# Softmax kept in PSUM, rotation finished in SBUF, and the work of five engines dealt out anew

## The reference

```python
xn = layernorm(x)
q, k, v = xn @ wq, xn @ wk, xn @ wv                 # 8 heads of 128
q, k = rope(q), rope(k)                             # halves: [e*cos - o*sin, e*sin + o*cos]
s = q @ k.T / 128 - 1e30 * (i < j)                  # causal
attn = softmax(s) @ v @ wo                          # summed over the heads
h = relu(s0 * [xn, -xn] @ sign(k0)) * 2             # 512 -> 1024
h = relu(s1 * h @ sign(k1)) * 2                     # 1024 -> 1024
out = x + attn + s2 * h @ sign(k2)                  # 1024 -> 256
```

## Time and profile before

| | us |
|---|---|
| median of three runs | 1775.95 (1774.67 to 1776.29) |
| the profiled execution | 1776.42 |
| its span, first to last instruction | 1774.5 |
| PE busy | 1721.9 (97%), 12720 matmuls |
| DVE busy | 1532.1 (86%) |
| ACT busy | 1267.3 (71%) |
| POOL busy | 927.4 (52%) |
| granted TensorE clock, mean | 0.996 of full speed |

### The profile page before, as it was taken

The page is one execution under the profiler, slowest core; times in us unless marked ns, Lnnn a source line. Parts: engine busy times, 40 slices in busy tenths (PEclk is TensorE's granted clock), DMA queues, the critical chain, the costliest instruction groups (busy, mean ns, idle before and its releaser), DMA issues.

```text
span 1774.5 us, 34051 instructions
## 1 busy us (share of the span) xinstructions
PE 1721.9 (97%) x12720; PEld 1195.5 (67%) x12720; DVE 1532.1 (86%) x3630; ACT 1267.3 (71%) x2717; POOL 927.4 (52%) x952
## 2 busy tenths in 40 slices
PE   6899989999999999999999999999999999999999
PEld 2456757767676676767767677676766767677667
DVE  7899888897988979888897988989889798888975
ACT  6677676776867777677776767768677776777763
POOL 6555545555545645464564555555456454655632
PEclk9999999999999999999999999999999999999999
DMA  4234543344343443344344343433434344343433
GB/s 172 48 48 79 93 68 79 66 78 76 63 92 58 87 70 64 86 67 85 59 79 89 63 81 66 78 72 66 87 65 88 67 65 85 67 87 58 80 70 73
DMA packets 454839, 134.09 MB, mean 76 GB/s; under 512 B 434704, under 2 KB 453648, under 8 KB 454672
## 3 DMA queue, kind: packets, MB, share of 16 engines
q1 hardware_dynamic: 454672, 131.90, 39.4%
HBM read 14.94 MB, written 8.39 MB: 13 GB/s over the span
## 4 chain that ended last, share of the span: by engine, by line
PE 68%; DVE 20%; POOL 3%; DMA 3%; ACT 3%; issue 2%; SPq 1%; DVEq 0%; POOLq 0%
PE bank L238 32%; PE bank L694 17%; PE bank L678 8%; PE bank L661 8%; DVE ph L584 3%; PE bank L705 3%; DVE bank L556 3%; DVE p L574 3%; DVE qk L559 2%; DVE bank L553 2%; DMA pt<-ph 2%; DVE rt L589 1%; POOL xT L342 1%; POOL tb L351 1%; ACT p L426 1%
## 5 line engine op out<-in xcount | busy, mean ns | idle before, releaser
L354 POOL TENSOR_SCALAR ph<-p,ri 128x384 f16<-128x384 f32 (+3 forms) x512 | 313.2, 612 | 455.4 <-DVE rk L581 418.2
L351 POOL TENSOR_TENSOR tb<-tb,sin 128x512 f32<-128x512 f32 x256 | 333.0, 1301 | 242.1 <-ACT tb L410 235.2
L694 PE MATMUL bank<-hb,wa 128*128 128x256 f16 x3360 | 379.9, 273 | 0.2 <-ACT bank L442 0.2
L694 PEld LDWEIGHTS bank<-hb,wa 128*128 128x128 fp8e5 x3360 | 328.0, 98 | 41.7 <-ACT bank L442 0.5
L426 ACT ACTIVATE p<-p,nm,sc 128x512 f32<-128x512 f32 (+3 forms) x512 | 328.5, 645 | 1.6
L584 DVE SCALAR_TENSOR_TENSOR ph<-p,rk,ph 128x512 f16<-128x512 f32 (+3 forms) x512 | 310.2, 613 | 0.7 <-POOL ph L354 0.7
L574 DVE CUSTOM_DVE_ANT_0 p<-bank,mask 128x512 f32<-128x512 f32 (+3 forms) x512 | 228.9, 484 | 48.9 <-PE bank L661 46.8
L661 PE MATMUL bank<-qk 128*128 128x512 f16 (+3 forms) x1536 | 231.6, 301 | 14.7 <-DVE qk L559 13.5
L678 PE MATMUL bank<-pt,v 128*128 128x256 f16 (+1 forms) x2304 | 232.5, 255 | 12.9 <-DMA pt<-ph 11.5
L678 PEld LDWEIGHTS bank<-pt,v 128*128 128x128 f16 x2304 | 202.5, 98 | 39.9 <-DMA pt<-ph 17.5
L661 PEld LDWEIGHTS bank<-qk 128*128 128x128 f16 x1536 | 133.3, 98 | 121.3 <-DVE qk L559 21.6
(11 more groups left out here) (111 smaller groups left out, 2266.3 us busy)
## 6 DMA issues: line engine op xcount, KB each, us to landing
out<-xnat SPq DMA_DIRECT2D x32, 256.0 KB, 2.4
xnat<-in_x SPq DMA_DIRECT2D x15, 512.0 KB, 3.9
pt<-ph SPq DMA_TRANSPOSE x256, 4.3
o<-in_k SPq DMA_DIRECT2D x1, 1024.0 KB, 7.4
v<-in_wq SPq DMA_DIRECT2D x1, 1024.0 KB, 9.4
v<-in_wk SPq DMA_DIRECT2D x1, 1024.0 KB, 11.1
ph<-in_wv SPq DMA_DIRECT2D x1, 1024.0 KB, 13.5
o<-in_wo SPq DMA_DIRECT2D x1, 1024.0 KB, 10.3
```

The costliest lines, as they stand in the source:

```text
L351: pool.tensor_tensor(tb, tb, SIN[:], ALU.mult).then_inc(s_crossed, 1)
L354: pool.tensor_scalar(part(g, i, HI), prob(g, i), RI[:, g % 4, i:i + 1], 4096.0, ALU.mult, ALU.mult).then_inc(s_P_hi, 1)
L694: mm = pe.matmul(ps[:, 256 * u:256 * u + 256], WA[:, w, k, (2 * j + u) * 128:(2 * j + u) * 128 + 128], HB[:, h, s, k, :], start=first and ...
```

## The change

- Scores stay in their bank. `row_max` writes back to the bank, `exponent` works in place there, and `p_hi` and `p_lo` read from there. The buffer P is gone; two small start-up tensors that lay in it now lie in PT. A bank with scores is free after `p_lo`, no longer after `row_max`.
- `p_hi` moves from POOL to ACT.
- `rotate` writes its sum to TB in SBUF. `qk_hi` (ACT) reads TB, and `qk_lo` moves from DVE to POOL. A bank with q or k is free after `rotate`. TB has four slots, not three.
- The lists of all engines are written anew, and the loop covers sequences 4 to 13 or 14 where it covered 2 to 14.

The code, with the beginning of the load order (the other lists differ in nearly every line):

```diff
--- before.py
+++ after.py
@@ -19,14 +19,14 @@
 EPS = 1e-5
 HI, LO = 0, 1
 WIDTH = [128 * (i + 1) for i in range(4)]
-S_OFF = {3: 0, 2: 512, 0: 896, 1: 1024}
+S_COL = {3: 0, 2: 0, 0: 384, 1: 0}
 S_FILLS = [(3,), (2, 0), (1,)]
 SQUARE = {3: (0, 0, 4), 2: (0, 1, 4), 1: (1, 0, 2), 0: (1, 1, 2)}
 SQ_AT = [0, 2048]
 SQ_SIZE = [1024, 512]
 PV_RUNS = [(0, 0, 2, 4), (1, 0, 2, 4), (2, 0, 2, 4), (3, 0, 3, 4), (0, 1, 0, 2), (1, 1, 1, 2)]
 ORING = 8
-TRING = 3
+TRING = 4
 
 
 PRODUCTS = {1: (0, 2), 2: (1, 0), 3: (6, 1), 4: (2, 6), 5: (3, 3), 6: (4, 5), 7: (5, 4)}
@@ -57,7 +57,6 @@
         TB = sb("tb", [128, TRING, T])
         V = sb("v", [128, 2, 4, 1024], F16)
         O = sb("o", [128, ORING, 2, T], F16)
-        P = sb("p", [128, 2, 1280])
         PH = sb("ph", [128, 2, 3072], F16)
         PT = sb("pt", [128, 2, 24, 128], F16)
         HB = sb("hb", [128, 7, 2, 4, 256], F16)
@@ -87,8 +86,9 @@
         H0 = flat[:, 0:8192].rearrange("p (s k n) -> p s k n", s=2, k=8)
         W1F = [flat[:, 8192:14336].rearrange("p (k n) -> p k n", k=6),
                RT[:, 4:8].rearrange("p a b -> p (a b)").bitcast(F16).rearrange("p (k n) -> p k n", k=2)]
-        AM = P[:, 1, 0:256].rearrange("p (i n) -> p i n", i=2)
-        ONES = P[:, 1, 256:384]
+        early = PT[:, 0, 0:6].rearrange("p a b -> p (a b)").bitcast(F32)
+        AM = early[:, 0:256].rearrange("p (i n) -> p i n", i=2)
+        ONES = early[:, 256:384]
         BANK = [ctx.enter_context(nc.psum_tensor(f"bank{i}", [128, 512], F32)) for i in range(8)]
 
 
@@ -218,8 +218,8 @@
         def quarter(v, n):
             return v.rearrange("p (c n) -> p c n", c=2)[:, :, n * 256:n * 256 + 256]
 
-        def prob(g, i):
-            return P[:, g % 2, S_OFF[i]:S_OFF[i] + WIDTH[i]]
+        def tile_of(ps, i):
+            return ps[:, S_COL[i]:S_COL[i] + WIDTH[i]]
 
         def part(g, i, s):
             q, row, n = SQUARE[i]
@@ -350,9 +350,9 @@
             tb = TB[:, (2 * g + w) % TRING, :]
             pool.tensor_tensor(tb, tb, SIN[:], ALU.mult).then_inc(s_crossed, 1)
 
-        def p_hi(pool, g, i):
-            pool.tensor_scalar(part(g, i, HI), prob(g, i), RI[:, g % 4, i:i + 1], 4096.0,
-                               ALU.mult, ALU.mult).then_inc(s_P_hi, 1)
+        def qk_lo(pool, g, w):
+            pool.tensor_tensor(QK[:, g % 2, 2 * w + 1, :], TB[:, (2 * g + w) % TRING, :], QK[:, g % 2, 2 * w, :],
+                               ALU.subtract).then_inc(s_qk_lo, 1)
 
         def h0t_lo(pool, i):
             pool.tensor_tensor(HB[:, 3:7, LO, i, :], RT[:, 4:8], HB[:, 3:7, HI, i, :], ALU.subtract).then_inc(s_h0t, 1)
@@ -409,8 +409,8 @@
             act.activation(TB[0:64, r, :], ps[64:128, :], ACT.Copy)
             act.activation(TB[64:128, r, :], ps[0:64, :], ACT.Copy).then_inc(s_swap, 1)
 
-        def qk_hi(act, g, w, ps):
-            act.activation(QK[:, g % 2, 2 * w, :], ps[:, :], ACT.Copy).then_inc(s_qk_hi, 1)
+        def qk_hi(act, g, w):
+            act.activation(QK[:, g % 2, 2 * w, :], TB[:, (2 * g + w) % TRING, :], ACT.Copy).then_inc(s_qk_hi, 1)
 
         def v_hi(act, grp, t, ps):
             act.activation(V[:, HI, t, grp * 512:grp * 512 + 512], ps[:, :], ACT.Copy,
@@ -422,9 +422,13 @@
         def row_bias(act, g):
             act.activation(NM[:, g % 4, :], MX[:, g % 4, :], ACT.Copy, scale=SC[:, 1:2]).then_inc(s_bias, 1)
 
-        def exponent(act, g, i):
-            act.activation(prob(g, i), prob(g, i), ACT.Exp, bias=NM[:, g % 4, i:i + 1], scale=SC[:, 0:1],
+        def exponent(act, g, i, ps):
+            p = tile_of(ps, i)
+            act.activation(p, p, ACT.Exp, bias=NM[:, g % 4, i:i + 1], scale=SC[:, 0:1],
                            accum_out=SM[:, g % 4, i:i + 1]).then_inc(s_exp, 1)
+
+        def p_hi(act, g, i, ps):
+            act.activation(part(g, i, HI), tile_of(ps, i), ACT.Copy, scale=RK[:, g % 4, i:i + 1]).then_inc(s_P_hi, 1)
 
         def keep_r(act, ps):
             act.activation(RT[:, 0:2].rearrange("p a b -> p (a b)"), ps[:, :], ACT.Relu).then_inc(s_r, 1)
@@ -553,11 +557,8 @@
             dve.tensor_tensor(ps[:, :], ps[:, :], COS[:], ALU.mult).then_inc(s_straight, 1)
 
         def rotate(dve, g, w, ps):
-            dve.tensor_tensor(ps[:, :], ps[:, :], TB[:, (2 * g + w) % TRING, :], ALU.add).then_inc(s_rot, 1)
-
-        def qk_lo(dve, g, w, ps):
-            dve.tensor_tensor(QK[:, g % 2, 2 * w + 1, :], ps[:, :], QK[:, g % 2, 2 * w, :],
-                              ALU.subtract).then_inc(s_qk_lo, 1)
+            tb = TB[:, (2 * g + w) % TRING, :]
+            dve.tensor_tensor(tb, ps[:, :], tb, ALU.add).then_inc(s_rot, 1)
 
         def v_lo(dve, grp, t, ps):
             a = grp * 512
@@ -570,8 +571,8 @@
                                      ALU.mult, ALU.subtract).then_inc(s_o, 1)
 
         def row_max(dve, g, i, ps):
-            a, w = {3: 0, 2: 0, 0: 384, 1: 0}[i], WIDTH[i]
-            dve.tensor_tensor_reduce(out=prob(g, i), in0=ps[:, a:a + w], in1=MASK[:, 512 - w:512], scale=1.0,
+            s = tile_of(ps, i)
+            dve.tensor_tensor_reduce(out=s, in0=s, in1=MASK[:, 512 - WIDTH[i]:512], scale=1.0,
                                      scalar=-3.0e38, op0=ALU.add, op1=ALU.max,
                                      accum_out=MX[:, g % 4, i:i + 1]).then_inc(s_max, 1)
 
@@ -580,8 +581,8 @@
             dve.wait_ge(s_recip, g + 1)
             dve.tensor_scalar(RK[:, g % 4, :], RI[:, g % 4, :], 4096.0, None, ALU.mult).then_inc(s_inv, 1)
 
-        def p_lo(dve, g, i):
-            dve.scalar_tensor_tensor(part(g, i, LO), prob(g, i), RK[:, g % 4, i:i + 1], part(g, i, HI),
+        def p_lo(dve, g, i, ps):
+            dve.scalar_tensor_tensor(part(g, i, LO), tile_of(ps, i), RK[:, g % 4, i:i + 1], part(g, i, HI),
                                      ALU.mult, ALU.subtract).then_inc(s_P_lo, 1)
 
         def difference(dve, n, ps):
@@ -724,36 +725,39 @@
 
 
...
         def sync_program(sp):
+            load_x_rest(sp)
             load_x_first(sp)
-            load_x_rest(sp)
+            load_k(sp, 0)
+            load_w(sp, "k")
+            load_w(sp, "q")
             load_scales(sp)
-            load_k(sp, 0)
             load_k(sp, 1)
-            load_w(sp, "q")
-            load_w(sp, "k")
-            load_cos(sp)
+            load_w(sp, "v")
             load_sin(sp)
-            load_k(sp, 2)
-            load_w(sp, "v")
-            load_x(sp, 1)
             sp.wait_ge(s_k0, 4)
             load_w(sp, "o")
+            load_cos(sp)
+            load_x(sp, 1)
+            load_k(sp, 2)
             sp.wait_ge(s_P_lo, 4)
             sp.wait_ge(s_pad, 1)
             turn_p(sp, 0)
...
```

7351 lines of the change are left out of this document (4725 added, 2626 removed), and 25 rows, old and new, of the table ROTATION.

## The result

The changed kernel takes 1762.13 us (median of four runs, 1761.06 to 1763.64) against 1775.31 (1774.62 to 1776.29) for the kernel before on the same chip: ratio 0.9927, 95% interval 0.9915 to 0.994. I predicted 1764. Its profiled execution, the slowest of its four, has a span of 1761.8 us, 12.7 less than before.

A forecast was written before the change was run, and what follows sets the result against it. PE was taken to be at its floor, 106.0 of 107.93 us per loop sequence. 1776.4 - 9 (loop) - 2 (start) - 1 (sequences 1 to 3; end 0) = 1764.4, median 0.5 lower: 1764 us, range 1746 to 1793.

The forecast's parts named there:

- The floor: PE's work in one loop sequence, priced by distances between matmul groups: 106.0 us, against 107.93 measured before the change.
- The price of `p_hi`: `p_hi` on ACT from a bank: 0.43 us in the mean, 13.7 us per sequence, bounds 0.25 and 0.59 us.
- DVE: DVE's busy time per loop sequence: 94.3 less 10.9 for `qk_lo` and 4.0 for `p_lo`, 79.4 us.
- The loop: PE's 1.9 us over its floor per sequence become 1.2: 9 us gained over 13; bounds 25 gained, 20 lost.
- one or two waits of 0.2 to 0.5 us in place of 1.07: PE's waits per loop sequence: shorter new ones replace 0.38 us for transposed probabilities and 0.69 us for `qk_lo`.
- its old cause: In the loop, the 0.69 us wait for `qk_lo` was to go with the order that made it.
- The start: Before the loop: first matmul from 8.1 to about 12.5 us, first head's scores about 53; net -2 us, bounds -10, +8.
- the wait of 2.95 us with its slow group: At the start, ahead of the second head's scores: this wait and 1.6 us of slow group need not come again.
- Between 180 us and sequence 2: Sequences 1 to 3 carry the same edits: -1 us; the loop's first rounds were counted in the loop's gain.
- The end: Between last scores and last `values` PE has 15.2 us, the softmax needs 10 and transposes some 4: 0 change.
- the named bank: Bank of head 8b + 6's tile 3, tightest in the loop: PE leaves 8.9 us, `p_lo` done at 8.9, some 0.5 left.
- The rival: Scores held in banks make PE wait in the loop: two or three 1 us waits per sequence, about 1789; chance 0.20.

The follow-up runs named there:

- e9: Changed kernel with the three moves of e5 and the constant of e2 (division by the row's sum left out): 1738.02 us, 0.9791 of the kernel before.
- e2: Changed kernel with `p_hi` and `p_lo` scaled by the constant 4096, not the per-row value (division by row sum left out): 1746.52 us, 0.9837 of the kernel before.
- e4: Changed kernel with ACT's `qk_hi` of k for head 8b moved behind the first of four exponentials in the loop: 1753.32 us, 0.9872 of the kernel before.
- e3: Changed kernel with an added 512-column ACT copy ahead of each head's first `p_hi`: 1807.53 us, 1.0175 of the kernel before.
- e8: Changed kernel with an added DVE instruction (one input in PSUM) ahead of each of 256 `straight`: 1806.86 us, 1.0175 of the kernel before.
- e6: Kernel before, with one `p_lo` in DVE's loop moved behind the second `qk_lo` of head 8b+1: 1770.84 us, 0.9977 of the kernel before.
- e5: Changed kernel with scales loaded third, the move of e4, and head 8's `qk_hi` and `qk_lo` moved earlier: 1749.58 us, 0.9855 of the kernel before.
- e7: Changed kernel with an added 512-column DVE instruction, SBUF inputs, behind each of 256 `rotate`: 1884.08 us, 1.0608 of the kernel before.

## Why the prediction was right

The forecast was 1764 and the time 1762.1, with the mechanism as named: DVE relieved, ACT the busiest behind PE, POOL unchanged, a loop a little nearer to PE's floor. But its terms were not right one by one. I had summed 7.7 us for the 11 periods, 2 for the start, 2.4 for what lies between (1, and the loop's first two rounds) and 0 for the end; measured are 3.9, 1.9, 5.2 and 1.7. That the sum hits within 2 us is luck: the loop gave half of its term, and waits that I had not looked at, with some help of the clock, gave the rest.

- **The floor, right.** 106.0 us per sequence; e9 runs at 106.11.
- **The price of `p_hi`, mis-sized.** 0.542 us in the mean, not 0.43, and under my upper bound of 0.59 for the mean. I took it from copies without a row-wise scale. e2 shows that scale to cost 0.08 to 0.09 us on ACT. A row of the same kernel had it: `split_w_hi` (L396), a copy with such a scale, takes 0.714 us at 512 columns from SBUF. The Trainium skill states it too ("ScalarE: Activation LUTs", section "What ACT_TABLE_LOAD costs": each operand that is a pointer to one value per partition adds about 93 ns), and the trace agrees. ACT still came out at 90.7 us, since exponentials became shorter (0.645 to 0.587, 1.9 us per sequence) and neighbours overlap: the four `p_hi` at 1095.23 take 1.80 us together where their durations add up to 2.17, 3 us per sequence.
- **DVE, mis-sized.** 84.4 us, not 79.4. `qk_lo` went as computed (10.9). `p_lo` gave 32 × (0.613 - 0.545) = 2.2, not 4.0. And `row_max`, which I took as unchanged, costs 0.514 instead of 0.484 with a read of the accumulator of 0.142 instead of 0.081, 32 × 0.091 = 2.9 against. What this is due to, its output in the bank or another thing, I did not test.
- **The loop, direction right and size wrong.** I expected the period to fall by 0.7 us; it fell by 0.36, 3.9 us over 11 periods where 7.7 were meant, and by 0.1 in a steady sequence. The failed step is "one or two waits of 0.2 to 0.5 us in place of 1.07": it is one wait, of 1.01, and not where I looked. I had followed the softmax to `p_lo`, which comes in time by 0.1 us. I had struck out `qk_lo` since its old cause was gone, and had not followed it through its new order: swap, `crossed`, `rotate`, four exponentials, `qk_hi`, POOL. e4 shows the wait to be only a matter of where `qk_hi` stands.
- **The start, right in sum, by luck.** -1.9 us to 180 us, where I had -2. The scales landed at 13.7 us and the first matmul came at 14.5, where I had 12.5; about half of the delay was absorbed, and the first head's scores start at 55.06, not 53. `layer1` was to wait 2 to 3 us for `p_lo`; its chains wait for nothing, and the nearest wait for `p_lo` is 0.63 us at 72.50. And the wait of 2.95 us with its slow group, which "need not come again", did come again, at head 8: 2.96 us, and 1.7 us of slow groups at half clock.
- **Between 180 us and sequence 2, missed.** 5.2 us, where I took 1 and 1.4 of the loop's. I had looked for waits in the loop and at the start only. Three waits of 5.16 us and a stretch at half clock stood in between.
- **The end, missed.** 1.7 us, where I took 0. Before has a wait of 1.47 us for transposed probabilities there (at 1707.94), which I had not listed. (The 6.5 us of projection in that sum are 60 matmuls, five heads and not 20; their price holds.)
- **The banks did not bind.** e3 says how near it was: with 0.64 us more on ACT per head the named bank waits, for 0.21 us, and the loop loses 2.8 us per sequence, mostly by what else is queued on ACT. The rival had two or three waits of 1 us for a softmax 1 us longer, 108.9 us per sequence; with less than that e3 has 110.2, with its larger waits at `h1_lo` and `qk_lo`. So the rival had the size too low and the place wrong.

What paid for the change is shown in part. The new order is not better by itself: with DVE's former load added to it, it is 1.8 us per sequence slower than the old one (109.62 against 107.80, e8), as far as an added instruction can stand for `qk_lo`. And the old order was not spent: one move brought it to the same mean period (e6), and to a shorter one in its steady sequences (107.12 against 107.41). The change relieved DVE of 10 us per sequence, gave ACT 12, and with the order in which it was dealt out kept most of the old loss in the loop. e4, e5 and e9 show what was left: 0.9 us per sequence for the place of one instruction, 0.5 for the row-wise scales.

Not settled: why e8 costs 44 us although most of its instruction lies beside `crossed`. By the traces 24 of these are in the 11 periods, 12 before them and 7 behind.

## What to carry to other kernels

When an engine is at its floor and the others are 80% busy or more, follow every operand that this engine waits for through the new order, not only the one that the change makes late: a wait removed by its old cause comes back by its new queue. Price an instruction with its scalar operands, from a row that has them. And list the waits of the whole span before summing, since prologues of a few sequences can hold as much as the loop.

## What the runs showed of the hardware

- An ACT copy with a scale read per row costs 0.08 to 0.09 us more than with a constant, at every width (e2), and `p_lo` on DVE 0.062 to 0.067 more.
- A DVE operation on 512 columns with two float32 inputs in SBUF takes 1.061 us beside a POOL that is half busy, with one input in PSUM 0.684 (e7, e8), and POOL's `qk_lo` rises from 1.163 to 1.242 with it. The Trainium skill ("SBUF — State Buffer", section "Who interferes with whom") has GpSimd share a port pair with such VectorE instructions, which would explain both; the runs show the sizes, not the port.
- A load of 1.5 KB behind five loads of 3 MB together in one queue landed 10.3 us after its issue, against 3.2 as third load; in e2, e3 and e4, with the same order, it took 8.8 to 9.7.
- The TensorE clock was granted at half for 3.4 us behind a wait of 2.96 us (after, 148.7 to 152.1 us) and for 3.4 behind one of 2.19 (before, 245.8 to 249.2); behind waits of 2.49 (e2) and of 2.26 and 2.95 (e6) it stayed at full speed. The executions of the kernel before differ by 2 to 3 us with it.
